# A graph kernel's attention takes its score maximum in one vector instruction, over the scores plus a bf16 edge mask that the first message step stores beside the edge counts

## The reference, cut to what matters

```python
h = x @ W.T
e = leaky_relu(h[src] @ a_src + h[dst] @ a_dst, 0.2)
seg_max = segment_max(e, src)
exp_e = exp(e - seg_max[src])
denom = segment_sum(exp_e, src)
attention = exp_e / denom[src]
h_prime = segment_sum(attention[:, None] * h[src], dst)
x = x + elu(h_prime)
```

## Time and profile before

| what | before |
|---|---|
| median of the runs | 7337.82 us |
| profiled execution's own time | 7338.52 us |
| its span | 7336.8 us |
| PE, DVE, ACT, POOL busy | 67%, 60%, 51%, 51% |
| mean granted clock of PE | 0.827 |
| matrix read back and counted (step 0) | about 1104 to 2786 us |
| steps 1 to 3 | about 2786 to 5694 us |
| attention's blocks | about 5829 to 6886 us |

### The profile page before, as it was taken

One profiled execution on the slowest core, in us unless ns is written; L12 is line 12 of the kernel. 1 busy time (PEld: TensorE's weight loads), 2 busy tenths in 40 slices (PEclk: granted clock), 3 DMA queues, 4 the chain that ended last, 5 costly groups with the idle time before them and its releaser, 6 DMA issues. The chain is left out here.

```text
span 7336.8 us, 96109 instructions
## 1 busy us (share of the span) xinstructions
PE 4935.3 (67%) x39375; PEld 2538.1 (35%) x39375; DVE 4431.9 (60%) x7733; ACT 3720.7 (51%) x2634; POOL 3759.0 (51%) x3297
## 2 busy tenths in 40 slices
PE   0110238774444458999889989899988377676678
PEld 0110114432222224555545555455554211111123
DVE  9889977654334445554455545445444599999700
ACT  0000009975555455665556656566655177777401
POOL 0017777777777755688764888638870000000230
PEclk9755559987777779999999999999999576767799
DMA  9920028884443355766557756466654233334398
GB/s 412 428 73 0 0 67 277 258 229 149 158 154 145 141 198 173 239 212 221 189 173 228 241 186 231 149 224 229 224 190 142 97 143 155 153 146 158 141 418 363
DMA packets 344782, 1415.02 MB, mean 193 GB/s; under 512 B 129310, under 2 KB 182836, under 8 KB 314516
## 3 DMA queue, kind: packets, MB, share of 16 engines
q1 hardware_dynamic: 159676, 1138.67, 42.6%
q10 hardware_dynamic: 79672, 239.96, 8.7%
q0 software_dynamic: 104992, 30.24, 3.2%
HBM read 1008.21 MB, written 400.36 MB: 192 GB/s over the span
## 5 line engine op out<-in xcount | busy, mean ns | idle before, releaser
L582 PE MATMUL ps_all<-ring,T 128*64 128x448 f16 x32928 | 3324.9, 363 | 840.3 <-ACT ring L745 686.1
L582 PEld LDWEIGHTS ps_all<-ring,T 128*64 128x64 bf16 x32928 | 1923.3, 113 | 2226.1 <-issue 798.5
L744 ACT ACTIVATE ring<-ring 128x3136 uint16<-128x3136 uint8 x502 | 1410.4, 2810 | 1676.8 <-DVE t L1077 861.5
L479 POOL DMA_INDIRECT R<-in_edge_attr,eid x1568 | 1893.2, 1207 | 664.9 <-issue 477.0
L447 POOL DMA_INDIRECT mat_d<-cT,idxT x1563 | 1685.3, 1078 | 965.4 <-ACT cT L686 489.2
L745 ACT ACTIVATE ring<-ring 128x3136 uint16<-128x3136 uint8 x502 | 1405.9, 2801 | 0.0
L1115 DVE SCALAR_TENSOR_TENSOR R<-R,ring 128x784 f32<-128x784 uint16 x392 | 363.3, 974 | 811.1 <-DMA csum_d<-R 727.4
L1671 POOL DMA_INDIRECT sg<-seg_d,endI x49 | 57.8, 1179 | 1208.9 <-POOLq L199 1194.3
L536 PE MATMUL ps_all<-ident,R 128*128 128x128 f32 x448 | 108.3, 422 | 809.2 <-DVE R L835 809.2
L1614 PE MATMUL ps_all<-ad,ones 3*128 3x384 bf16 (+1 forms) x686 | 320.7, 467 | 343.4 <-ACT ps_all L1584 342.7
L1590 ACT ACTIVATE L<-ps_all,bias 128x384 f32<-128x384 f32 (+1 forms) x686 | 425.9, 621 | 148.7 <-PE ps_all L1614 145.4
(11 more groups left out here) (372 smaller groups left out, 3887.3 us busy)
## 6 DMA issues: line engine op xcount, KB each, us to landing
ring<-mat_d SPq DMA_DIRECT2D x784, 784.0 KB
C<-csum_d SPq DMA_DIRECT2D x98, 3136.0 KB, 15.5
mat_d<-ring SPq DMA_DIRECT2D x98, 1568.0 KB, 39.6
csum_d<-R ACTq DMA_DIRECT2D x196, 784.0 KB
seg_d<-R ACTq DMA_DIRECT2D x32, 1568.0 KB
msg_d<-t ACTq DMA_DIRECT2D x196, 128.0 KB
R<-in_edge_attr,eid POOLq DMA_INDIRECT x1568
mat_d<-cT,idxT POOLq DMA_INDIRECT x1563
```

The lines of the kernel that those rows point to most:

```text
L479: pool.indirect_dma_start(slab[n % 2][:, c, 0:FA], None, attr, bass.IndirectOffsetOnAxis(eid[:, at:at + 1], 0)).then_inc(s_at[n % 2], 16)
L582: mm = pe.matmul(accs[h * D:(h + 1) * D, j, 0:GW], lhsT, ring[:, n % 6, h * HQ + j * GW:h * HQ + (j + 1) * GW], start=first, stop=True, sk ...
L744: act.activation(to[:, 0, :], two[:, 0, :], ACT.Copy)
```

## The change

A second matrix `edge_d`, of bf16, is kept in device memory: 0 where the count is not zero, and -1e30 where the count is zero. In step 0 DVE makes it from each quarter of the counts, two instructions of 784 columns, into two buffers MK that lie in memory free in that step; ACT stores it behind the quarter's counts. A quarter now waits for the landing of both stores of the quarter two before it. Where POOL corrects a count, it also writes a zero into `edge_d`. The attention's `largest(s)` reads the mask M instead of the counts, and adds it to `ad` and takes the maximum in one instruction. The counts have three buffers instead of four there, and are waited for in `weighted`.

```diff
@@ -52,6 +52,7 @@
 UNIT = 2.0 ** 24
+NONE = -1.0e30
 BPS = NB + 2
@@ -258,6 +259,8 @@
         csum = csum_d[0:NP * NP, :].rearrange("(r c) a -> r (c a)", c=NP)
+        edge_d = nc.dram_tensor("edge_d", (NP * NP + P, 1), BF16).ap()
+        edges = edge_d[0:NP * NP, :].rearrange("(r c) a -> r (c a)", c=NP)
         key2_d = nc.dram_tensor("key2_d", (P * SW,), I32).ap()
@@ -302,6 +305,8 @@
             s_cso = sems(ph, t + "sumout0", t + "sumout1")
+            s_mko = sems(ph, t + "maskout0", t + "maskout1")
+            (s_mk,) = sems(ph, t + "masked")
             (s_eva, s_evd, s_gt, s_sg, s_tt, s_tn, s_h) = sems(ph, *(t + n for n in (
@@ -313,6 +318,7 @@
             one8 = sb(ph, "one8", [P, 1], U8)
+            zero16 = sb(ph, "zero16", [P, 1], BF16)
             eid = sb(ph, "eid", [P, EC], I32)
@@ -324,6 +330,7 @@
             re = flat[:, 0:NX * D].rearrange("p (k m) -> p k m", m=D)
+            MK = [flat[:, 512 + k * (QW // 2):512 + (k + 1) * (QW // 2)].bitcast(BF16) for k in range(2)]
             r32 = flat[:, 4 * GW + 5 * P + NX * D:4 * GW + 5 * P + NX * D + KT * D]
@@ -458,6 +465,7 @@
                     pool.wait_ge(s_cso[k], 16 * NB * NQ // 2)
+                    pool.wait_ge(s_mko[k], 16 * NB * NQ // 2)
                 for n in range(NS):
@@ -465,13 +473,15 @@
                             if j:
-                                pool.wait_ge(s_cw, 16 * j)
+                                pool.wait_ge(s_cw, 32 * j)
                             pool.indirect_dma_start(e1["now"][:, :], None, csum_d,
...
                                                     e1["now"][:, :], None).then_inc(s_cw, 16)
+                            pool.indirect_dma_start(edge_d, bass.IndirectOffsetOnAxis(i1["to"][:, :], 0),
+                                                    zero16[:, :], None).then_inc(s_cw, 16)
                     if n and n % PER == 0 and n // PER < STEPS - 1:
@@ -479,7 +489,7 @@
                 gathered(STEPS - 1)
-                pool.wait_ge(s_cw, 16 * NSG)
+                pool.wait_ge(s_cw, 32 * NSG)
 
@@ -750,6 +760,8 @@
                         act.dma_start(csum[c * P:(c + 1) * P, o * QW:(o + 1) * QW], CS[o % 2]).then_inc(s_cso[o % 2], 16)
+                        act.wait_ge(s_mk, c * NQ + o + 1)
+                        act.dma_start(edges[c * P:(c + 1) * P, o * QW:(o + 1) * QW], MK[o % 2]).then_inc(s_mko[o % 2], 16)
 
@@ -764,6 +776,9 @@
                     contracted(st, act)
+                    if st == 0:
+                        for k in range(2):
+                            act.wait_ge(s_mko[k], 16 * NB * NQ // 2)
                     for j in range(NG):
@@ -913,6 +928,7 @@
                 dve.memset(one8[:, :], 1)
+                dve.memset(zero16[:, :], 0.0)
                 dve.memset(srcK[0:1, 0:1], -1.0)
@@ -1110,12 +1126,18 @@
                             dve.wait_ge(s_cso[o % 2], 16 * (n // 2))
+                            dve.wait_ge(s_mko[o % 2], 16 * (n // 2))
                         for h in range(2):
...
                         ad.then_inc(s_csm, 1)
-                    dve.wait_ge(s_csm, (c + 1) * NQ)
+                        dve.wait_ge(s_csm, n + 1)
+                        for h in range(2):
+                            at = slice(h * sumW, (h + 1) * sumW)
+                            mk = dve.tensor_scalar(MK[o % 2][:, at], CS[o % 2][:, at], 0.0, NONE, ALU.is_equal, ALU.mult)
+                        mk.then_inc(s_mk, 1)
+                    dve.wait_ge(s_mk, (c + 1) * NQ)
                     dve.tensor_reduce(cn_src[:, c:c + 1], rs[:, :], AX.X, ALU.add).then_inc(s_csr, 1)
@@ -1479,12 +1501,14 @@
             with Phase() as ph:
-                s_ld = sems(ph, *(f"n_load{k}" for k in range(4)))
+                s_ld = sems(ph, *(f"n_load{k}" for k in range(3)))
+                s_ml = sems(ph, *(f"n_mask{k}" for k in range(2)))
                 (s_rd, s_one, s_clr, s_v, s_b, s_r, s_u, s_e, s_pr, s_hd, s_mm, s_m, s_x, s_o, s_tn, s_on) = sems(
                     ph, *("n_" + n for n in ("dots", "ones", "cleared", "dve", "biases", "positive", "leaky", "exp", "weighted", "scaled", "counted",
                                              "below", "elu", "out", "turned", "nodes")))
                 ad = sb(ph, "ad", [P, NP])
-                C = [sb(ph, f"C{k}", [P, NP]) for k in range(4)]
+                C = [sb(ph, f"C{k}", [P, NP]) for k in range(3)]
+                M = [sb(ph, f"M{k}", [P, NP], BF16) for k in range(2)]
                 L = [sb(ph, f"L{k}", [P, NP]) for k in range(2)]
@@ -1517,10 +1541,15 @@
                         sp.dma_start(ad3[32 * g:32 * g + 3, 0:to - at], dot3_d[:, at:to]).then_inc(s_rd, 16)
-                    for s in range(NB):
-                        if s >= 4:
-                            sp.wait_ge(s_mm, s - 3)
-                        sp.dma_start(C[s % 4][:, :], csum[s * P:(s + 1) * P, :]).then_inc(s_ld[s % 4], 16)
+                    for s in range(-1, NB):
+                        if s + 1 < NB:
+                            if s >= 1:
+                                sp.wait_ge(s_b, s)
+                            sp.dma_start(M[(s + 1) % 2][:, :], edges[(s + 1) * P:(s + 2) * P, :]).then_inc(s_ml[(s + 1) % 2], 16)
+                        if s >= 0:
+                            if s >= 3:
+                                sp.wait_ge(s_mm, s - 2)
+                            sp.dma_start(C[s % 3][:, :], csum[s * P:(s + 1) * P, :]).then_inc(s_ld[s % 3], 16)
 
@@ -1538,11 +1567,10 @@
                         t = L[s % 2][:, :]
-                        dve.wait_ge(s_ld[s % 4], 16 * (s // 4 + 1))
+                        dve.wait_ge(s_ml[s % 2], 16 * (s // 2 + 1))
                         if s >= 2:
                             dve.wait_ge(s_pr, 2 * (s - 1))
-                        link(dve.scalar_tensor_tensor(t, C[s % 4][:, :], 1.0, ad[:, :], ALU.min, ALU.mult))
-                        link(dve.tensor_reduce(md[:, :], t, AX.X, ALU.max))
+                        link(dve.tensor_tensor_reduce(t, M[s % 2][:, :], ad[:, :], 1.0, 0.0, ALU.add, ALU.max, accum_out=md[:, :]))
                         link(dve.tensor_scalar(e1[:, :], md[:, :], as1[:, s:s + 1], -1.0, ALU.add, ALU.mult))
@@ -1550,7 +1578,9 @@
                         for k, part in enumerate(parts):
-                            c = C[s % 4][:, part]
+                            c = C[s % 3][:, part]
+                            if k == 0:
+                                dve.wait_ge(s_ld[s % 3], 16 * (s // 3 + 1))
                             dve.wait_ge(s_e, s * NU + NU // 2 * (k + 1))
@@ -1619,7 +1649,7 @@
                                 j = k - NU // 2
-                                mm = accumulated(pe, HD[(s - 1) % 2][:, :], C[(s - 1) % 4], s == 1 and j < 6, j, j + 1)
+                                mm = accumulated(pe, HD[(s - 1) % 2][:, :], C[(s - 1) % 3], s == 1 and j < 6, j, j + 1)
                         if s:
```

## The result

| | before | after |
|---|---|---|
| median of 20 runs each, one chip | 7344.28 us (7329.18 to 7367.98) | 7364.64 us (7349.18 to 7486.9) |
| profiled execution | 7338.52 us | 7363.51 us |

The ratio is 1.0025, 95% interval 1.0017 to 1.0033. That is 18 us more (12 to 24). It is under the 0.3% that the prediction named as hard to tell from none, but with 20 runs on each side it is told: the interval leaves no room for a gain. The forecast was +12 us. A few runs, as the one of 7486.9 us here, fell in a slower state that both kernels have, and every ratio of this text leaves them out. The profiled execution of before lies 6 us under its median and that of after 1 us under its own, which is most of what separates 25 from 18.

The account below looks back on a forecast made before the run. The prediction held DVE (21.3 us a block) and the ACT-PE chain (20.3) nearly level in the attention. From 7338.5 us, -51 (attention) + 39 (scatter) + 19 (end of step 0) + 5 (steps 1 to 3) = +12: 7350 us, range 7325 to 7375.

Parts of the forecast that it names:

- the end of step 0: After the scatter: last masks, quarters' stores and the last mask store add 19 us, between 7 and 30.
- The bound of the attention: Attention: ACT's chain with PE, 20.34 us a block, limits once DVE is faster; gain 51 us.
- The new instruction: Attention: one maximum instruction over 6272 columns takes 6.7 us, replacing two of 6.68 and 6.69 us.
- The slow maximum: Rival, attention: new maximum runs at the scan's rate, attention loses some 5 us; +68, 7406 us; chance 0.07.
- the fast clock: Rival, attention: PE meets its fast level more often, two thirds of ACT's 145.4 us go; 7250 us; chance 0.05.
- The mask instructions: Step 0, DVE: eight per block of 784 columns, about 0.55 us each, 4.0 us a block.
- Heavy masks: Rival, step 0: masks run at one column per cycle and hold POOL at 0.21; +57, 7395 us; chance 0.20.
- The scatter: Step 0: DVE's masks slow POOL by 0.84 us a block over 46 blocks, +39 us.
- Light masks: Rival, step 0: masks cost POOL no more than the sort did, 9 us; total -22, 7316 us; chance 0.25.
- The rate of 0.21: Step 0: POOL loses 0.21 us per us of DVE's busy time.
- The early part: Step 0, 1104 to 1656 us: ACT a few us later per block, hidden as blocks catch up with the scatter.
- Steps 1 to 3: POOL's eight more transfers take 10.4 us, half counted: +5 us, between 0 and 10.

Follow-up runs that it names:

- e11: Kernel before with neither of the maximum's two passes, the softmax shift coming from 64 columns of the counts; ratio 0.9965 (0.9915 to 1.0014), slow chip.
- e5: Kernel before with the maximum taken in one instruction over count times score, no mask, sum's floor 1e-30; 7314.85 us, ratio 0.994.
- e7: Changed kernel with masks made in step 0 but neither stored nor scattered, attention reading bytes of the counts; 7357.48 us, ratio 0.9993.
- e8: Changed kernel with no masks made or scattered, ACT storing as many bytes taken from the counts; 7329.69 us, ratio 0.996.
- e6: Changed kernel with the attention of the kernel before, so masks are made, stored, scattered and never read; ratio 1.0072, +53 us.
- e1: Changed kernel without its part in step 0, attention loading bytes of the counts as mask; ratio 1.0021 (0.9935 to 1.0106), slow chip.
- e2: Same kernel as e6, the changed kernel with the attention of the kernel before, on a slow chip; ratio 1.0414.
- e4: Same kernel as e8, the changed kernel with stores of count bytes and no masks, on a slow chip; ratio 1.0271.
- e9: Changed kernel with every mask instruction of step 0 done twice; ratio 1.1092 (1.1031 to 1.1153), slow chip.
- e10: Changed kernel without POOL's eight scatters of zeros into the masks; between 9253.88 and 10232.33 us, slow chip.
- e3: Same kernel as e7, the changed kernel with masks made but neither stored nor scattered, on a slow chip; ratio 0.9427.
- e12: Changed kernel with ACT's wait for last mask stores moved behind the feature copies, POOL's to its first zero scatter; 9777.0 us, slow chip.

## Why the prediction was right, point by point

The mechanism was right in its main parts: what the attention gains and why, and that the masks hold POOL's scatter back by about as much. That the sum came within 6 us of the runs is in part luck, since the end of step 0 came out nearly right from the wrong cause and errors of 4 to 8 us stand on either side.

- **The bound of the attention** (chain of ACT and PE, 20.34 us a block) was right, shown by e11: without any pass of the maximum the block is as long as with one. Predicted -51, measured -47 in the profile and -44 (33 to 54) in e5's time. The 44.5 us of waits went. What the missing 4 us are isn't settled: ACT waits 2.6 us longer for PE (148.0 against 145.4), but 8.7 longer in e5 (154.1), whose stretch is the same.
- **The new instruction** at the rate of the two removed ones: 6.7 us foreseen, 6.684 measured. The slow maximum falls (its price was also put too low: 13.55 - 13.37 = 0.18 us more a block is 9 us, not 5). So does the fast clock: 0.66 granted against 0.69, and PE's waits unchanged. The rule of the Trainium skill cited with it ("DVE: opcode table, instruction layouts, handler registers and perf-mode slots", section "Datapath and trigger behaviour"), that a stage reading its own last result runs without a bubble, agrees with this 6.684 us; the scan's rate would have made 13.55.
- **The mask instructions**: 0.55 us foreseen, 0.568 at the median. Heavy masks fall.
- **The scatter**: +39 foreseen, 44.0 later measured. By the pace, 1121 transfers times 0.034 us, it is 38; 4 fewer issued by 1104 us make 6 more. The masks' own part is 35 us (e7). Light masks, 9 us, fall. The rate of 0.21 was close: 35 us over 46 blocks of 8 times 0.568 us is 0.17 us of POOL per us of DVE. But where DVE works matters as much as how much: the early part, called hidden, moved DVE's counting from the second stretch to the third. One step of the reasoning was too simple. It put all of POOL's excess down to DVE's busy time, but e8 has DVE busy for as long as e5 from 1104 to 2697 us (763.3 and 759.7 us) and still scatters 17 us later by the pace.
- **The early part** was the largest miss that cost little. I expected "a few us later per block"; 7 blocks fell behind, with one stall of 94.07 us. The slack took it: of 445.9 us of waits 206.5 are left. As this used up 239 us, as much again would be more than is left; the blocks would then set the end of step 0 themselves, which no run here shows.
- **The end of step 0**: +19 foreseen, +15 measured, from the wrong cause. Some 10 us were put down to the masks DVE still has to make, 5 to the quarters' stores, and 4 to the last masks and the last store together. e7 and e8 turn this round: 2 for the masks, 14 for the stores. To step 1's first gather, the distance that the prediction named, it was 87.8 us and is 104.5, +17. The last store's landing, put at 5 us, delays the copy by 2.96.
- **Steps 1 to 3** were mis-sized: +5 foreseen, half of the 10.4 us of the eight transfers; 13.5 measured between the profiles, and 19.2 between e6 and e5. Both kernels that scatter zeros take 2870 us and before, e5 and e7 2852 to 2856. But e8, which doesn't, takes 2838.7, so single executions differ by as much; the signs are POOL's longer idle time beside the scatter of zeros (33.0 against 22.0 us), which the term left out, and its gathers, which took 2715.3 us from the first start to the last and 2703.6 before; that all of POOL's lateness comes through is likely and not shown.
- **The sum**: +12 foreseen, +18 (12 to 24) measured, +25 between the profiles. Against the profiles, 4 in the attention, 8 in steps 1 to 3 and 5 in the scatter were missing, and 4 were too many at the end of step 0.

## What to carry to other kernels

Before a pass is taken from the busiest engine, find the second chain: the gain is the difference of the two, and here a pass of 6.7 us a block was worth 0.8 in the steady part. What is prepared elsewhere for the faster pass must be cheaper than that difference, and its price includes the time that other engines lose beside it, here POOL, which makes no mask. If a cheaper bound will do in place of an exact value (e5), the preparation isn't needed at all.

## What the runs showed of the hardware

- A running maximum over two operands takes 6.684 us for 6272 columns, with a bf16 or an f32 first operand.
- POOL's issue of indirect transfers is slower where DVE works more, and not by DVE's work alone: from 1656 to 2697 us the mean is 810.71 / 757 = 1.071 us with DVE busy for 404.15 us (e5), 814.59 / 744 = 1.095 with 499.52 (e7), 820.07 / 725 = 1.131 with 630.09 (after), but 816.15 / 739 = 1.104 with only 460.20 in e8, which stores and makes no masks. In the sort before 1104 us the same program issued 446 transfers in one execution and 423 in another (e5), 1014 and 1086 ns each.
- In five of the eight profiles on the two slow chips (e1, e2, e4, e9, e10) PE and POOL fell into step in the scatter. From 1656 to 2697 us PE ran 374 to 765 matmuls there, at a granted clock of 0.50 to 0.53, beside some 761 transfers of POOL. In the other three (e3, e11, e12) it ran 5269 to 5945, and in the changed kernel 5048. So it isn't a matter of the chip alone; e10's own times, from 9253.88 to 10232.33 us, suggest that it changes from execution to execution. From e9, in order of time:

```profile
2299.79 1.10 POOL L454 DMA_INDIRECT mat_d<-cT,idxT  x1 [0.30 <-issue]
2300.91 0.53 PE L592 MATMUL ps_all<-ring,T 128*64 128x448 f16 x1 [2.27 <-issue]
2301.19 1.10 POOL L454 DMA_INDIRECT mat_d<-cT,idxT  x1 [0.30 <-issue]
2302.30 0.13 PEld L592 LDWEIGHTS ps_all<-ring,T 128*64 128x64 bf16 x1 [2.67 <-issue]
```

PE gets one instruction, a weight load or a matmul, for each of POOL's transfers, 1.40 us apart, and waits for nothing that the profile shows. After the scatter's last start, at 2777.8 us, PE works the blocks off: 7652 matmuls from 2778 to 4130 us. In all, its weight loads of this line stood 2980.1 us for "issue" in e9 and 804.8 in e5 (L582 there). Which of the two holds the other, and why on these chips, stays open. The ratios of these chips go from 0.9427 (e3, out of step) to 1.1092 (e9, in step) and so say nothing of the change.
